# A four-layer graph network on one core: who asks for the weights and edges, and whether the node stages clear their input tiles

## What is computed

```
for layer in (L0, L1, L2, L3):
    h = relu(layernorm(x))          # per node, 256 features
    x = x + layer(h, src, dst, edge values)
# L0: h @ W.T + b, scaled to unit length times a sigmoid gate; softmax over the edges of a target; expmap0
# L1: segment_sum(edge_weight * (h @ w_nbr)[src], dst) + h @ w_own + bias
# L2: score of each edge from two projections, softmax over the edges of a source, weighted sum, @ W_fc.T
# L3: two projections to 64 features mixed by edge_attr_2, 4 heads, softmax over the edges of a target
```

## Time and profile before

| | |
|---|---|
| median of 3 runs | 7770.79 us (7767.35 to 7773.11) |
| the profiled execution | 7767.28 us |
| span of its profile | 7765.6 us |
| mean granted TensorE clock | 0.912 |
| busy share PE / DVE / ACT / POOL | 75% / 67% / 41% / 50% |

### The profile page before, as it was taken

One profiled execution on the slowest core, in us unless ns is written; L12 is line 12 of the kernel. 1 busy time (PEld: TensorE's weight loads), 2 busy tenths in 40 slices (PEclk: granted clock), 3 DMA queues, 4 the chain that ended last, 5 costly groups with the idle time before them and its releaser, 6 DMA issues. The chain is left out here.

```text
span 7765.6 us, 152919 instructions
## 1 busy us (share of the span) xinstructions
PE 5835.2 (75%) x23114; PEld 3640.4 (47%) x23115; DVE 5212.0 (67%) x18189; ACT 3200.1 (41%) x8779; POOL 3879.1 (50%) x4972
## 2 busy tenths in 40 slices
PE   4997999847779997777999967777686779400477
PEld 3774344336634443554444445555335668300365
DVE  5999777745579995456666666666784569533765
ACT  1993355304445552244444444554222457300044
POOL 1556777700022223766767677777460013577443
PEclk7999999979999998899999989999899999755799
DMA  1664333559967775787889866666208978422177
GB/s 58 212 210 131 99 107 100 167 164 329 320 211 249 246 248 199 244 303 261 310 309 311 295 197 203 204 203 203 62 7 283 340 249 229 130 55 55 48 237 249
DMA packets 918627, 1560.30 MB, mean 201 GB/s; under 512 B 123789, under 2 KB 635005, under 8 KB 918502
## 3 DMA queue, kind: packets, MB, share of 16 engines
q1 hardware_dynamic: 602758, 860.67, 33.6%
q10 hardware_dynamic: 188000, 410.91, 15.0%
q0 software_dynamic: 127744, 287.44, 13.7%
HBM read 861.17 MB, written 697.48 MB: 201 GB/s over the span
## 5 line engine op out<-in xcount | busy, mean ns | idle before, releaser
L2130 PE MATMUL node_p_out<-w,node_h_t 128*128 128x512 f32 (+2 forms) x6272 | 2175.7, 469 | 12.8 <-ACT node_h_t L2166 11.1
L1434 PE MATMUL merge_banks<-merge_rows,merge_mask 128*128 x6264 | 1538.5, 400 | 533.9 <-SPq L1365 156.2
L1434 PEld LDWEIGHTS merge_banks<-merge_rows,merge_mask 128*128 128x128 f32 x6264 | 1194.5, 197 | 877.9 <-issue 718.3
L1416 DVE TENSOR_SCALAR merge_mask<-ramp,dst_at,soft_at_step 128x128 f32<-128x128 f32 x2349 | 823.0, 353 | 776.5 <-PE merge_banks L1434 622.6
L2130 PEld LDWEIGHTS node_p_out<-w,node_h_t 128*128 128x128 f32 x6272 | 1012.0, 190 | 455.0 <-issue 397.5
L2043 POOL TENSOR_TENSOR node_inv_std<-node_var,node_minus_half 128x4 f32<-128x4 f32 x392 | 433.3, 1105 | 1413.6 <-DVE node_var L1928 843.0
L1497 ACT COPY merge_total<-merge_banks 128x1024 f32<-128x1024 f32 x392 | 396.8, 1012 | 1245.9 <-PE merge_banks L1434 1235.6
L2166 ACT ACTIVATE node_h_t<-node_p_turn 128x256 f32<-128x256 f32 x1568 | 601.3, 383 | 217.9 <-PE node_p_turn L2108 211.9
L2108 PE MATMUL node_p_turn<-ident,node_xn 128*128 128x128 f32 x2352 | 466.4, 280 | 134.5 <-DVE node_xn L1999 95.7
L2056 POOL DMA_INDIRECT src_sorted<-node_key,node_key_at x392 | 446.2, 1138 | 182.2 <-issue 95.8
L2108 PEld LDWEIGHTS node_p_turn<-ident,node_xn 128*128 128x128 f32 x2352 | 298.5, 141 | 459.6 <-issue 201.4
(11 more groups left out here) (566 smaller groups left out, 11330.5 us busy)
## 6 DMA issues: line engine op xcount, KB each, us to landing
merge_held<-own ACTq DMA_DIRECT2D x196, 512.0 KB, 5.9
x<-merge_total ACTq DMA_DIRECT2D x196, 512.0 KB, 4.3
node_x<-x SPq DMA_DIRECT2D x196, 512.0 KB, 6.6
pair<-node_out SPq DMA_DIRECT2D x98, 1024.0 KB, 4.3
node_x<-in_x SPq DMA_DIRECT2D x194, 512.0 KB
merge_rows<-h_by_edge SPq DMA_DIRECT2D x408, 128.0 KB, 3.6
merge_rows<-by_edge SPq DMA_DIRECT2D x408, 128.0 KB, 3.7
h<-node_rows_h SPq DMA_DIRECT2D x98, 516.0 KB, 4.2
```

The lines of the kernel that those rows point to most:

```text
L1416: ins = nc.vector.tensor_scalar(mask[j][:], k.ramp[:, 0:P], columns(k.dst_at, s), columns(weight, s), ALU.is_equal, ALU.mult)
L1434: nc.tensor.matmul(banks[:, bass.ds(nc.s_assert_within(at[2 * j + 1], 0, (BANKS - 1) * 512, skip_runtime_bounds_check_because=small), D)], ...
L2130: ins = nc.tensor.matmul(p_out[w][g % banks][:, 0:n], h_t[g][:, c * P:(c + 1) * P], matrix[:, c, :], start=c == 0, stop=c == 1)
```

## The change

Two things are moved and one is removed.

1. The tiles that the weights' and the edges' transfers write to are allocated in a phase of their own (`asked`), which stays open over `constants`, `weights` and `load_edges`. ScalarE asks for the 25 transfers of the weights in the block of `constants`, with no wait in front. SyncE asks for the 24 transfers of the edges in the same block, behind the five fills that it needs; GpSimd's three fills stand in front of its own constants there, and VectorE's two clears in front of its own.
2. `weights` and `load_edges` keep only what comes after the landing.
3. The node stages don't clear `x`, and SyncE doesn't wait for `preset` in them. GpSimd waits for the small constants alone.

```
-def constants(nc, k):
+def constants(nc, k, w, e):
...
         @block.gpsimd
         def _(pool):
+            B = k.TC // P
+            nc.gpsimd.iota(e.prev_i[:], pattern=[[P * P, B]], base=-1, channel_multiplier=P).then_inc(e.preset, 1)
+            for t in e.raw_i:
+                nc.gpsimd.iota(t[:], pattern=[[P * P, B], [1, P]], base=0, channel_multiplier=P).then_inc(e.preset, 1)
             nc.gpsimd.memset(k.ones[:], 1.0).then_inc(filled, 1)
...
+        @block.scalar
+        def _(act):
+            for to, frm in w.asked:
+                act.dma_start(to, frm, allow_slow_non_contiguous=True).then_inc(w.landed, 16)
+
+        @block.sync
+        def _(sp):
+            e.ask(sp)
+
         @block.vector
         def _(dve):
+            nc.vector.memset(e.raw[2][:], 0.0).then_inc(e.preset, 1)
+            nc.vector.memset(e.pair[:], 0.0).then_inc(e.preset, 1)
             nc.vector.memset(k.pos_i[:], 0).then_inc(s_done, 1)
...
+    def ask(sp):
+
+        sp.wait_ge(preset, 5)
+        for at_rows, b, cols, at, n, w in runs():
+            ...                      # the same 24 dma_start as in load_edges before
...
@@ node_pass
-            sp.wait_ge(preset, S)
             pipeline(sp, groups, ([(0, load)] if layer == 1 else []) + [(0, load_x), (store_lag, store_tables)], apart=2)
...
-            for h in range(S):
-                nc.vector.memset(x[h][:], 0.0).then_inc(preset, 1)
             nc.vector.memset(minus_half[:], -0.5).then_inc(preset, 1)
...
-            pool.wait_ge(preset, S + (2 if layer == 1 else 1))
+            pool.wait_ge(preset, 2 if layer == 1 else 1)
...
@@ weights
-        @block.sync
-        def _(sp):
-            for to, frm in loads + thin:
-                sp.dma_start(to, frm, allow_slow_non_contiguous=True).then_inc(landed, 16)
...
@@ gnn_kernel
-        constants(nc, k)
-        weights(nc, k, a)
-        load_edges(nc, k, a, sorted_rows)
+        asked = Phase(nc, "asked")
+        w, e = weight_tiles(nc, k, a, asked), edge_tiles_in(nc, k, a, asked)
+        constants(nc, k, w, e)
+        weights(nc, k, w)
+        load_edges(nc, k, e, sorted_rows)
+        asked.close()
```

More of the change, by code:

```diff
@@ L96, in constants, with edge_tiles_in @@
     ph.close()
-def load_edges(nc, k, a, rows):
-    ph = Phase(nc, "load")
-    E, TC, B = k.E, k.TC, k.TC // P
+def edge_tiles_in(nc, k, a, ph):
+    e = Asked()
+    E, B = k.E, k.TC // P
     raw_i = [ph.sb(f"raw_i{n}", [P, B, P], I32) for n in range(2)]
@@ L107, in load_edges @@
     pair = ph.sb("pair", [P, B, P, 2])
[L108 to L116, removed]
+    prev_i = ph.sb("prev_i", [P, B], I32)
+    preset, landed = ph.sem("edges_preset"), ph.sem("edges_landed")
     full, rest = E // P, E % P
@@ L134, in load_edges @@
     n_landed = 64 * len(list(runs())) + 16 * len(list(before_runs()))
-    with nc.Block() as block:
[L136 to L140, removed]
+    def ask(sp):
+        sp.wait_ge(preset, 5)
+        for at_rows, b, cols, at, n, w in runs():
+            for field, t in ((a["src"], raw_i[0]), (a["dst"], raw_i[1]), (a["edge_weight"], raw[2])):
+                sp.dma_start(t[at_rows, b, cols], field[at:at + n * w].rearrange("(n w) -> n w", w=w)).then_inc(landed, 16)
+            sp.dma_start(pair[at_rows, b, cols, :].rearrange("n w c -> n (w c)"),
+                         a["edge_attr_2"][at:at + n * w, :].rearrange("(n w) c -> n (w c)", w=w)).then_inc(landed, 16)
+        for at_rows, b, lo, hi in before_runs():
+            sp.dma_start(prev_i[at_rows, b:b + 1],
+                         a["dst"][(lo - 1) * P:(hi - 1) * P].rearrange("(n w) -> n w", w=P)[:, P - 1:P],
+                         allow_slow_non_contiguous=True).then_inc(landed, 16)
@@ new lines, in edge_tiles_in, with load_edges @@
+    e.raw_i, e.raw, e.pair, e.prev_i, e.preset, e.landed, e.n_landed, e.ask = raw_i, raw, pair, prev_i, preset, landed, n_landed, ask
+    return e
+def load_edges(nc, k, e, rows):
+    ph = Phase(nc, "load")
+    E, TC, B = k.E, k.TC, k.TC // P
+    raw_i, raw, pair, prev_i, landed, n_landed = e.raw_i, e.raw, e.pair, e.prev_i, e.landed, e.n_landed
+    row_form = ph.sb("row_form", [P, B, P, 5])
+    prev = ph.sb("prev", [P, B])
+    falls, most = ph.sb("falls", [P, B, P]), ph.sb("most", [P, 1])
+    any_fall = ph.sb("any_fall", [1, 1])
+    p_falls = ph.ps("p_falls", [P, 512])
+    part = [ph.sb(f"part{n}", [P, B, P]) for n in range(2)]
+    turned = [ph.ps(f"turned{n}", [P, B * P]) for n in range(5)]
+    cast, turn, s_done = (ph.sem(n) for n in ("cast", "turn", "done"))
+    step, summed, rows_made, rows_put = (ph.sem(n) for n in ("step", "summed", "rows_made", "rows_put"))
+    with nc.Block() as block:
@@ L142, in _ @@
         @block.sync
         def _(sp):
[L144 to L153, removed]
             sp.wait_ge(rows_made, 5)
@@ L162, in _ @@
         def _(dve):
-            nc.vector.memset(raw[2][:], 0.0).then_inc(preset, 1)
-            nc.vector.memset(pair[:], 0.0).then_inc(preset, 1)
             dve.wait_ge(landed, n_landed)
@@ L2719, in head_shares, with weight_tiles @@
     hold.close()
-def weights(nc, k, a):
-    ph = Phase(nc, "weights")
+class Asked:
+    pass
+def weight_tiles(nc, k, a, ph):
+    w = Asked()
     square = [ph.sb(f"square{n}", [P, 2, D]) for n in range(4)]
@@ L2730, in weights @@
     attn3 = ph.sb("attn3", [64, 4])
[L2731 to L2736, removed]
+    landed = ph.sem("weights_landed")
     loads = [(square[n][:], a[name].rearrange("(d p) i -> p d i", p=P)) for n, name in enumerate(names)]
@@ L2750, in weights @@
     thin += [(attn3[:, n:n + 1], a["L3_gnn_attn_forward"][0, n:n + 1, :].rearrange("o p -> p o")) for n in range(4)]
+    w.square, w.flat, w.attn0, w.bias0, w.attn3, w.landed, w.asked = square, flat, attn0, bias0, attn3, landed, loads + thin
+    return w
+def weights(nc, k, w):
+    ph = Phase(nc, "weights")
+    square, flat, attn0, bias0, attn3, landed = w.square, w.flat, w.attn0, w.bias0, w.attn3, w.landed
+    bias_rows = ph.sb("bias_rows", [P, 2, P])
+    spread_out = ph.sem("spread_out")
+    p_turn = [ph.ps(f"p_turn{n}", [P, 512]) for n in range(4)]
+    p_flat = ph.ps("p_flat", [P, 512])
+    p_attn = ph.ps("p_attn", [P, 512])
+    turned, s_done = ph.sem("turned"), ph.sem("done")
     with nc.Block() as block:
-        @block.sync
-        def _(sp):
-            for to, frm in loads + thin:
-                sp.dma_start(to, frm, allow_slow_non_contiguous=True).then_inc(landed, 16)
         @block.tensor
         def _(pe):
-            pe.wait_ge(landed, 16 * len(loads + thin))
+            pe.wait_ge(landed, 16 * len(w.asked))
             for n in range(4):
@@ L2782, in _ @@
         def _(dve):
-            dve.wait_ge(landed, 16 * len(loads + thin))
+            dve.wait_ge(landed, 16 * len(w.asked))
             nc.vector.tensor_tensor(k.both_bias[:], k.own_bias[:], k.fc_bias[:], ALU.add).then_inc(s_done, 1)
```

## The result

The changed kernel takes 7743.16 us (median of 6 runs, 7732.27 to 7745.63) against 7770.52 (6 runs, 7767.35 to 7777.67). The ratio is 0.9959, with a 95% interval of 0.9947 to 0.9970: 32 us faster by the ratio (23 to 41), 27.4 us by the medians. The forecast was 7738, in a range of 7728 to 7752. The profiled execution of the changed kernel has a span of 7740.1 us and a mean granted clock of 0.914; before it was 7765.6 and 0.912.

A forecast was written before the change was run, and what follows sets the result against it. No engine bounds the whole; phases wait at their edges, at the start mostly for DMA issue time. Start 15.6 plus node stages 16.6 gave 32.2 us off 7770.79, forecast 7738, range 7728 to 7752.

The forecast's parts named there:

- The node stages' 16.6 us: Fronts of four node stages: without clears the first load goes out 4.16 us earlier in each, 16.6 us together.
- The start's 15.6 us: Program start: VectorE enters the edges' phase at 27.17 instead of 42.79, gaining 15.6 us, 2.88 of it from the weights.
- The 25 issues take the 13.01 us that SyncE needs: Weights' train at the start: ScalarE issues from 1.01 to 14.02, landing 2.26 us later at 16.28 instead of 19.16.
- no slowing: Joint issuing at the start: ScalarE's and SyncE's trains keep their usual pace side by side; start's gain bounded at 5.5 us.
- the weights' own work: Start, between the weights' landing and VectorE's next phase: assumed to stay 10.89 us.
- The covers: Constants' block: added fills and clears end constants near 4.8 us, hidden behind ScalarE's train until 14.0; uncovered they cost 1.6.
- One maker of descriptors: Rival, 8%: at the start SyncE's and ScalarE's issues take turns; gain 22.1 us, time 7748.7.
- The fronts' cover: Rival, 5%: at node stage fronts something else behind the clears takes the same 4 us; gain 15.6, time 7755.2.
- the plan's clock: Rival, 6%: TensorE's clock stays low in the plan, up to 18.0 us more; gain 14.2, time 7756.6.
- the slower case: Rival, 4%: layer 1's TensorE-bound node stage runs longer at the low clock; 100 us of it gives 7788.
- The prediction's own sign: Last node stage: its start was to come 28.1 us earlier than 6338.45, at 6310.
- what moves without being touched: Later phases shift by up to 32 us; plan's clock may change it by +18.0 to −11.4, taken as 0.

The follow-up runs named there:

- e1: Changed kernel with the four clears of x and SyncE's wait put back in each node stage; ratio 0.9984 to the kernel before, 12.4 us under.
- e2: Kernel before without the node stages' clears of x and SyncE's wait for them, start as before; ratio 0.9980, 15.5 us under.
- e7: Kernel before plus 25 tiny unread transfers issued by ScalarE in the weights' block; one run, 7746.69 us.
- e3: Changed kernel, but SyncE asks for the edges in the weights' block, after ScalarE's train; repeat beside the changed kernel: ratio 0.9966 to the kernel before.
- e8: Changed kernel with weights' and edges' transfers split between ScalarE and SyncE, thin single-element ones first; repeat: ratio 0.9961 to the kernel before.
- e4: Changed kernel with ScalarE and SyncE each asking for every second weights' and edges' transfer; issues took 9.14 us, weights landed at 15.16.

## Why the prediction held, and which term was off

**The mechanism.** In the traces both changes did what the prediction said: the edges' wait disappears behind the weights' work, and the node stages start with their load. e1 and e2 measure the parts by themselves, 12.4 us (5 to 19) and 15.5 us (7 to 23), for 15.6 and 16.6 forecast; both agree, but neither is sharp (see e7 and the remainder).

**The node stages' 16.6 us** came out at the fronts as summed. At all four, the trace shows SyncE's load beside VectorE's first constant, and e2's time agrees (15.5, 7 to 23).

**The start's 15.6 us were 11.4.** The step that was mis-sized is "The 25 issues take the 13.01 us that SyncE needs ... Landing as before 2.26 us later: 16.28". Measured were a train of 16.05 us and a landing at 18.62: 2.3 us of the 4.2 that are missing. The prediction had worked out that the DMA engines would have 13.2 us of work, had concluded that this would cost 0.2 us, and took "no slowing" from a row of seven issues. The sum of work was right (a mean share of 0.66 over the first 20 us of the trace after is 13.2 us), but it took the engines as evenly loaded from 1.0 on. They were full from 6 to 12 us, the issues of both sequencers stretched in that time, and the single-element transfers at the end of ScalarE's list then still had to be issued one by one. That the edges beside them are the cause is shown by e3: without them the weights land at 16.59. That the issues stretch because the engines are full is only argued, as e8 and e2 have full engines with issues at their usual pace.

The other 1.9 us are the weights' own work: the prediction shifted it unchanged, 10.89 us from the landing to VectorE's next phase, and it took 12.81 (31.43 − 18.62). The small matmuls ran at the slow pace. Of 13 other traces, 6 have the fast pace and 7 the slow, in no relation to when TensorE began (15.0 to 19.2 us in the fast ones, 14.9 to 19.8 in the slow), and e8 has one of each. The prediction had named TensorE's clock as what moves by itself, but only in the plan; there it took nothing: from the plan's start to the first node stage it is 69.7 before and 65.7 after, which is the front's 4.

**The covers.** GpSimd's and VectorE's added fills were hidden behind the trains as forecast: VectorE's last constant ends at 4.3 us, ScalarE's train at 16.9.

**The rivals.** One maker of descriptors is refuted by e4 (25 issues in 9.14 us). The fronts' cover, the plan's clock and the slower case did not come. (In the last, 65 / 2 is 32.5 and not 32.2; nothing hangs on it.)

**The remainder.** The two traces differ by 25.5 us: 11.4 from the start, 16.6 from the fronts, and 2.5 given back by all the rest. That remainder is a sum of larger ones of both signs. Net of its 4.16 us of clears, the way from node stage 1 to node stage 2 became 7.8 us shorter and node stage 2 11.0, while the first and third merge took 4.7 and 2.7 more, the last 5.9 and the sources' shares in layer 2 4.2. None of these stages has a changed instruction behind its front. The last merge depends on the program, not on the execution: 483.8 to 484.7 in three kernels with the old place of the fills, 487.4 to 491.0 in all eleven traces with the new one. In which engine's code, in which semaphore or tile the cause lies wasn't separated; that it is the place of code in memory is only a guess. What makes node stage 2 differ stays open too. So the agreement of 27.4 with 28.0 us rests in part on such shifts cancelling: that is luck. The prediction's own sign shows it too. The last node stage was to begin at 6310 and its first load goes out at 6309.54, though the start had given 4.2 us less than the sum says; untouched stages made up for it, and the last merge took back 5.9. The spread of "a few us" that the prediction allowed for what moves without being touched was for the plan's clock; single stages elsewhere moved by up to 11 us.

## What to carry to other kernels

Where a trace shows engines waiting for a train of DMA issues, putting the train behind work that exists anyway can remove that whole wait (12.74 us here); but a second train beside it can be slowed (13.0 to 16.1 us here), so look at how full the DMA engines are in the busiest us, not at the mean, and at how many single elements the transfers carry. A clear that only the first use of a buffer sees costs its whole time where the first load waits for it. With phases behind barriers, parts can be measured one by one; but this program answers with shifts of up to 11 us per stage that belong to neither part, and a better start of 4 us couldn't be shown in the total. A kernel with an addition that does nothing (e7) is a useful control: it says how much of a gain may be such a shift, and it should be run as often as the others.

## What was not expected

- During the small matmuls the granted clock of the trace reads 1.00, with the fast pace and with the slow. The pace of equal matmuls (256 or 357 ns for the same shape) says otherwise. The 16 transposes before them take 3.6 to 3.7 us with either pace; only what follows differs. With the fast pace a lower clock is recorded soon behind them (a mean of 0.62 from 20 to 30 us in e8); in the changed kernel, with the slow pace, it reads 1.00 until about 40 us, though 12 transposes of its edges take 2.82 us, as long as in the kernel before, where the record says 0.50. That no change was recorded there because none took place is only argued; in this stretch the column can't be read as TensorE's clock. Two traces of one program (e8, and e8 again), each with the window of the weights' transposes and matmuls:

```profile
15.00:21.90 6.90, 6.86 (x40) 6.30 (x40) 0.80 (x4) 0.00 (x0) 0.00 (x0) 1.00 0.37 101
```

```profile
15.00:24.00 9.00, 8.93 (x40) 8.32 (x40) 0.75 (x4) 0.00 (x0) 0.00 (x0) 1.00 0.29 79
```

- The last merge repeats within 0.1 us between two kernels that differ only in the clears (483.8 and 483.9), and is 5 to 6 us longer in kernels that differ in the first 30 us of the program.
- GpSimd's issue of the same scatter takes 1.14 us in the kernel before and in e2, and 1.01 to 1.03 in all others, e7 among them.
